# Storing the result of a two-layer cross-head convolution in 64 stores of 1 MB instead of 128 of 512 KB

## The chip, the cores and the metric

The kernel runs on one core of a Trainium2 chip. The metric is the time of one execution on the device in microseconds, as the median of several runs. The engines that matter are PE (matrix multiplications, with PEld loading its weights), DVE, ACT and POOL (element-wise work) and SP, which here only issues transfers. All transfers go through one queue of the core's 16 DMA engines.

## What is computed

The input x has 16 channels of 1024 rows (t) by 1024 columns (s), all in f32. Two layers of the same form follow each other, each with its own weights:

```
wI  = w + eye(16)
ret = einsum('MTS,MN->NTS', x, wI)                      # channels mixed
hq  = einsum('MTS,TIM->ITS', x, qw1);  ret += einsum('ITS,TIM->MTS', hq, qw2)   # rank 2, weights by row
hk  = einsum('MTS,SIM->ITS', x, kw1);  ret += einsum('ITS,SIM->MTS', hk, kw2)   # rank 2, weights by column
ret += x * qdd[t] + x * kdd[s]
```

So each layer applies a 16 x 16 matrix that depends on the row (T) plus one that depends on the column (S) to the channels. 64 MB are read and 64 MB are written.

## The kernel before

The image is worked on in 8 blocks (`BLOCKS`) of 128 rows. A block lies in SBUF as 16 chunks (`CHUNKS`) of 8 rows; a chunk is 128 partitions x 1024 f32, which is 4 KB in each partition and 512 KB in all. X holds the block's input and later the result of the first layer, Y holds sums on their way. Each layer has a pass by rows (T) and a pass by columns (S). The names in the code are t1 and s1 for the passes of the first layer, s2 and t2 for those of the second.

PE goes through them in a fixed order. For block k there is first the S stage: 16 groups of s1 (line 748) with those of s2 (line 767) two groups behind. Then comes the T stage: for each o in 0 to 15 the t2 products of output chunk o (line 796, two groups) and, right behind, t1 of chunk o of the next block k+1 (line 725). After t1 of chunk 15 the next block's S stage begins. PE waits for `x_loaded[j]` before t1 of chunk j (line 712). In the last block there is no t1, as there is no further block.

ACT moves the t1 sums from PSUM to Y (line 454) and the s2 sums to X (line 462). For each output chunk it also copies two half-tiles of X into OUT, which swaps the two halves of the partitions (`cross`, line 486). DVE adds the s1 sums to Y (line 614), makes every second weight tile of t2 (line 243) and adds the t2 sums into OUT in two instructions per chunk (`add_rows`, line 638), the second of which needs the crossed copies. POOL makes other weight tiles.

OUT has 4 slots (`OUT_SLOTS`); output chunk o uses slot o % 4. Before ACT's crossing of chunk o (line 483) and before DVE's first add of it (line 621) each waits until the store of chunk o - 4 has landed. Each slot has a semaphore `stored[n]`.

SP issues everything in program order. In the T stage (`t_phase`, line 319) it waits for each o until the adds of output chunk o are done, stores it (line 265), and loads chunk o + 3 of the next block (line 261, `SLACK` is 3) into the place that this output chunk has freed. After o = 11 it also issues the two stores of the next block's products of row weights (line 281, 128 KB each in runs of 64 bytes) and a load of row parameters (line 277); then follow o = 12, whose load is that of chunk 15, and the stores 13 to 15. Chunks 0 to 2 of the next block are loaded in the S stage (line 317), where nothing is stored; 16 loads of row weights RT are issued there as well (line 284).

Output chunk o holds rows of chunk (o + 3) % 16 (`t2_chunk`).

Of the kernel before, what the change touches and what calls it, by code (L numbers as in the profile page):

```python
# [4 lines left out]
P = 128  # L5
CH = 16
T, S = 1024, 1024
HALVES = 2
HALF = P // HALVES
PARTS = HALF // CH  # L10
EIGHTHS = HALVES * PARTS
COLS = S // EIGHTHS
WIDE = COLS // HALVES
ROWS = 128
BLOCKS = T // ROWS
RANK = 2
LAYERS = 2
PAIR = 2
PAIRS = ROWS // PAIR
CHUNK = 8  # L20
CHUNKS = ROWS // CHUNK
CHUNK2 = CHUNK // PAIR
SLACK = 3
# [5 lines left out]
PER_CHUNK = CHUNK // FEW  # L29
# [3 lines left out]
OUT_SLOTS = 4  # L33
# [16 lines left out]
QUARTERED_LAST = ()  # L50
PARAMS = 2 * RANK * CH + CH
DMA = 16
FLAT = CHUNK * COLS
BANK = 512
T1_COPIES = 2
# [5 lines left out]
def cross_conv_kernel(nc, x, first_rows, row_params, col_left, col_right0, col_right1, w, products, out):  # L61
# [15 lines left out]
    with ctx:  # L77
# [3 lines left out]
        def sem(name):  # L81
            return ctx.enter_context(nc.semaphore(name))
# [4 lines left out]
        OUT = sb("OUT", [P, OUT_SLOTS, CHUNK2, COLS, PAIR])  # L87
# [62 lines left out]
        a_done = sem("a_done")  # L150
        b_full = sem("b_full")
        b_done = sem("b_done")
        stored = [sem(f"stored{n}") for n in range(OUT_SLOTS)]


        def t1_groups(k):
# [21 lines left out]
        def t2_done(k):  # L178
            return (S1_ADDS * GROUPS + T2_GROUPS) * k + S1_ADDS * GROUPS
# [32 lines left out]
        def t2_chunk(o):  # L212
            return (o + SLACK) % CHUNKS
# [45 lines left out]
        def _(sp):  # L259
            def load_x(k, j):  # L260
                sp.dma_start(rows_of(X, k, j).rearrange("q a s c -> q (a s c)"),  # L261
                             x[bass.ds(k * CHUNKS + j, 1)].rearrange("b q v -> (b q) v")).then_inc(x_loaded[j], DMA)

            def store(k, o):
                sp.dma_start(out[bass.ds(k * CHUNKS + t2_chunk(o), 1)].rearrange("b q v -> (b q) v"),  # L265
                             OUT[:, o % OUT_SLOTS].rearrange("q a s c -> q (a s c)")
                             ).then_inc(stored[o % OUT_SLOTS], DMA)

            def load_right(h):

                for p in range(EIGHTHS):
                    sp.dma_start(KR1[h][CH * p:CH * (p + 1)].rearrange("q i s n -> q (i s n)"),  # L272
                                 col_right1[h, p:p + 1].broadcast_to([CH, RANK * SIDE * CH])
                                 ).then_inc(right_loaded[1 + h], DMA)

            def load_q(step):
                sp.dma_start(QP[:, :, :].rearrange("q l v -> q (l v)"),  # L277
                             row_params[bass.ds(step, 1)].rearrange("b t v -> (b t) v")).then_inc(q_loaded, DMA)

            def store_products(place, src, signal):  # L280
                sp.dma_start(products[bass.ds(place, 1)].rearrange("b c t n -> (b t) c n"), src).then_inc(signal, DMA)  # L281

            def load_part(place, l, p, first_row, rows, signal):
                sp.dma_start(RT[CH * p:CH * (p + 1), l, first_row:first_row + rows].rearrange("q t n -> q (t n)"),  # L284
                             products[bass.ds(place, 1), :, first_row:first_row + rows]
                             .rearrange("b c t n -> (b c) (t n)")).then_inc(signal, DMA)

# [30 lines left out]

            def t_phase(k, more, params):
                for o in range(CHUNKS):  # L320
                    sp.wait_ge(b_done, t2_done(k) + PER_CHUNK * (o + 1))
                    store(k, o)
                    if more and o + SLACK < CHUNKS:
                        load_x(k + 1, o + SLACK)
                    if more and o == PROD_STORE:
                        sp.wait_ge(prod_ready, LAYERS * (k + 2))
                        for l in range(LAYERS):
                            store_products(LAYERS * (k + 1) + l, PROD[:, l, 0], prod_stored)
                        if params:
                            load_q(k + 2)  # L330
# [118 lines left out]
        @block.scalar  # L449
        def _(act):  # L450
            def t1_copies(k, j):
                act.wait_ge(a_full, t1_groups(k) + j + 1)
                for h in range(HALVES):
                    nc.scalar.activation(  # L454
                        rows_of(Y, k, j)[:, :, WIDE * h:WIDE * (h + 1), :].rearrange("q a s c -> q a c s"),
                        PA[HALVES * (j % RING) + h][:, :].rearrange("q (a c s) -> q a c s", a=CHUNK2, c=PAIR),
                        ACT.Copy).then_inc(a_done, 1)

            def s2_copies(k, g):
                act.wait_ge(a_full, s2_groups(k) + g + 1)  # L460
                for i in range(HALVES):
                    nc.scalar.activation(columns_of(block_of(X, k), slice(0, P), WIDE * i + NARROW * g),  # L462
                                         by_columns(PA[HALVES * (g % RING) + i][:, :]), ACT.Copy
                                         ).then_inc(a_done, 1)

            def s1_matrices(k, g):

                act.wait_ge(b_full, s1_groups(k) + g - SLOTS + 1)
                if first(k):
                    act.wait_ge(mask_ready, 3)  # L470
                    act.wait_ge(right_done, UNITS)
                slot = WB[:, g % SLOTS].rearrange("q (t a n) -> q t a n", t=INDEX, a=PARTS)
                for a in range(PARTS):
                    nc.scalar.activation(slot[:, :, a, :], RS[:, 0, INDEX * g:INDEX * (g + 1)], ACT.Copy,  # L474
                                         scale=mask[:, a:a + 1]).then_inc(wb_act, 1)

            def cross(k, o):

                if o in quartered(k):
                    return  # L480
                if not (first(k) and o < OUT_SLOTS):

                    act.wait_ge(stored[o % OUT_SLOTS], DMA * (CHUNKS // OUT_SLOTS * k + o // OUT_SLOTS))
                lower, upper = slice(0, HALF), slice(HALF, P)
                for dst, src in ((lower, upper), (upper, lower)):
                    nc.scalar.activation(OUT[dst, o % OUT_SLOTS, :, WIDE:COLS, :],  # L486
                                         rows_of(X, k, t2_chunk(o))[src, :, WIDE:COLS, :], ACT.Copy
                                         ).then_inc(crossed, 1)

            def base(l):  # L490

                for n in range(CH):
                    nc.scalar.activation(RS[:, l, :, n:n + 1].rearrange("q s n -> q (s n)"), KL[:, l, RANK], ACT.Identity,
                                         bias=WI[:, l, n:n + 1], scale=delta[:, n:n + 1]).then_inc(base_ready, 1)

            def block_copies(k, more):
                s1_matrices(k, SLOTS)
                for g in range(GROUPS):
                    if g + LAG + SLOTS in ACT_S1:
                        s1_matrices(k, g + LAG + SLOTS)  # L500
                    s2_copies(k, g)

                act.wait_ge(a_done, t1_done(k + 1))
                cross(k, 0)
                for o in range(CHUNKS):
                    if more:
                        t1_copies(k + 1, o)
                    if o + 1 < CHUNKS:
                        cross(k, o + 1)

            act.wait_ge(wi_ready, LAYERS)
            for l in range(LAYERS):
                base(l)
            for j in range(CHUNKS):
                t1_copies(0, j)
            block_copies(0, True)
            with act.Fori(1, BLOCKS - 1) as k:
                block_copies(k, True)
            block_copies(BLOCKS - 1, False)

        @block.vector
        def _(dve):
# [94 lines left out]
            def add_rows(k, o):  # L617
                dve.wait_ge(b_full, t2_groups(k) + PER_CHUNK * (o + 1))
                if not (first(k) and o < OUT_SLOTS):

                    dve.wait_ge(stored[o % OUT_SLOTS], DMA * (CHUNKS // OUT_SLOTS * k + o // OUT_SLOTS))
                slot, place = OUT[:, o % OUT_SLOTS], rows_of(X, k, t2_chunk(o))
                banks = PBS[:, HALVES * (o % RING):HALVES * (o % RING + 1)]
                for i in range(HALVES):
                    def rows(chunk):
                        return chunk[:, :, WIDE * i:WIDE * (i + 1), :].rearrange("q a s c -> q a c s")

                    if o in quartered(k):
                        sums = banks[:, i].rearrange("q (a c s) -> q a c s", a=CHUNK2, c=PAIR)
                    else:  # L630
                        sums = banks.rearrange("q b (a c s) -> q (b a) c s", a=FEW2, c=PAIR
                                               )[:, :, :, WIDE * i:WIDE * (i + 1)]
                    other = place
                    if i and o not in quartered(k):

                        dve.wait_ge(crossed, crossings(k, o + 1))
                        other = slot
                    nc.vector.tensor_tensor(rows(slot), sums, rows(other), ALU.add).then_inc(b_done, 1)  # L638
# [247 lines left out]
```

## Time and profile before

| | |
|---|---|
| median of 3 runs | 790.45 us (783.79 to 791.59) |
| profiled execution | 784.83 us, its span 783.0 us |
| PE busy | 687.3 us (88%) |
| DVE, ACT, POOL busy | 541.5, 499.1, 485.2 us (69%, 64%, 62%) |
| mean granted PE clock | 0.962 of full speed |
| DMA | 159.08 MB, mean 203 GB/s; the queue's packets take 63.3% of the 16 engines' span |
| chain that ended last | PE 65%, SP's queue 9%, DMA 9%, issue 8%, DVE 7% |

The chain's share says which work stood on the path that set the end. A wait is told by who waited and what released it. "Issue" is time in which an engine waited for nothing that the profile shows. The landing time of a transfer is counted from its issue by SP until all of it has landed. In the slices of the span the DMA's busy share swings between nearly 0 and 9 tenths: the T stages carry the loads of x and all the stores, the S stages little.

### The profile page before, as it was taken

The page shows a single profiled execution, that of the slowest core. Times are in us where ns is not written, and L with a number is a line of the kernel's source. Part 1 is how long each engine was busy: PE and PEld are TensorE (multiplying, and loading weights), DVE is VectorE, ACT ScalarE, POOL GpSimd, SP SyncE. Part 2 cuts the span into 40 slices and gives each one's busy share as a digit, 9 for nine tenths or more (in the row PEclk, how much of TensorE's full clock was granted, in tenths as well). Part 3 has the DMA queues.
Part 4 walks back from the last instruction along what each step waited for, and adds up shares of the span by engine and source line. Part 5 has one row for each costly group of instructions (what it writes and reads, how often), then busy time and mean ns, then how long its engine had stood idle before and what let it go on. Part 6 is the DMA issues. An engine that isn't in the chain of part 4 may idle for free.

```text
span 783.0 us, 42554 instructions
## 1 busy us (share of the span) xinstructions
PE 687.3 (88%) x18448; PEld 634.9 (81%) x18448; DVE 541.5 (69%) x769; ACT 499.1 (64%) x929; POOL 485.2 (62%) x456
## 2 busy tenths in 40 slices
PE   7378899888998999988998989979999789988976
PEld 2368889887887888978897988969989779988975
DVE  4375667475875758756785667757786567957797
ACT  7246577565776667755776657757777557765753
POOL 2257777566665766657765666647866467656632
PEclk9669999999999999989999899999999999999999
DMA  7982559942896529855499437975399545992055
GB/s 165 204 283 58 138 200 340 270 112 77 310 324 198 132 83 349 269 185 144 157 339 265 126 111 269 315 231 129 111 355 277 175 132 188 335 272 61 9 210 215
DMA packets 78567, 159.08 MB, mean 203 GB/s; under 512 B 42048, under 2 KB 43072, under 8 KB 76224
## 3 DMA queue, kind: packets, MB, share of 16 engines
q1 hardware_dynamic: 78408, 156.59, 63.3%
q8 instruction: 146, 2.39, 1.3%
q14 instruction: 13, 0.11, 0.0%
HBM read 87.22 MB, written 69.34 MB: 200 GB/s over the span
## 4 chain that ended last, share of the span: by engine, by line
PE 65%; SPq 9%; DMA 9%; issue 8%; DVE 7%; ACT 0%; DVEq 0%; ACTq 0%
PE PB L796 22%; PE PB L748 15%; PE PA L767 14%; PE PA L725 14%; DMA X<-in_x_dram 8%; SPq L281 5%; DVE OUT L638 3%; DVE WB L243 2%; DVE Y L614 2%; SPq L277 1%; SPq L265 1%; SPq L272 1%; SPq L284 1%; DMA products<-RT 1%; SPq L261 1%
## 5 line engine op out<-in xcount | busy, mean ns | idle before, releaser
L796 PE MATMUL PB<-Y,WB 128*128 128x128 f32 x2048 | 268.8, 281 | 9.5 <-DVE OUT L638 8.2
L796 PEld LDWEIGHTS PB<-Y,WB 128*128 128x128 f32 x2048 | 242.4, 188 | 22.7 <-issue 15.4
L614 DVE TENSOR_TENSOR Y<-PB,Y 128x512 f32 (+1 forms) x256 | 165.1, 689 | 107.4 <-PE PB L748 88.2
L454 ACT ACTIVATE Y<-PA 128x512 f32<-128x512 f32 (+1 forms) x256 | 146.5, 631 | 132.3 <-PE PA L725 132.1
L243 POOL TENSOR_TENSOR WB<-RT,mask 128x512 f32<-128x512 f32 x128 | 143.0, 1117 | 111.4 <-PE PB L796 107.7
L725 PE MATMUL PA<-X,WA 64*64 64x64 f32 x8192 | 165.2, 231 | 45.5 <-DMA X<-in_x_dram 24.9
L462 ACT ACTIVATE X<-PA 128x512 f32 (+1 forms) x256 | 140.4, 606 | 98.4 <-PE PA L767 98.3
L725 PEld LDWEIGHTS PA<-X,WA 64*64 64x64 f32 x8192 | 146.1, 143 | 64.9 <-DMA X<-in_x_dram 27.5
L235 POOL TENSOR_TENSOR WA<-RS,mask 128x512 f32<-128x512 f32 x128 | 133.5, 1043 | 85.4 <-PE PA L767 53.2
L748 PE MATMUL PB<-X,WB 64*64 64x128 f32 x4096 | 162.8, 281 | 19.7 <-issue 14.1
L235 POOL TENSOR_TENSOR WA<-RT,mask 128x512 f32<-128x512 f32 x128 | 140.2, 1098 | 61.6 <-PE PA L725 27.2
L486 ACT ACTIVATE OUT<-X 64x512 f32<-64x512 f32 (+1 forms) x256 | 161.1, 629 | 20.3 <-DMA out_dram<-OUT 13.7
L767 PE MATMUL PA<-Y,WA 64*64 64x128 f32 x4096 | 157.9, 274 | 10.8 <-issue 10.6
L243 DVE TENSOR_TENSOR WB<-RT,mask 128x512 f32<-128x512 f32 x128 | 111.5, 871 | 75.7 <-PE PB L796 43.4
L748 PEld LDWEIGHTS PB<-X,WB 64*64 64x64 f32 x4096 | 140.1, 138 | 26.4 <-issue 26.3
L767 PEld LDWEIGHTS PA<-Y,WA 64*64 64x64 f32 x4096 | 136.2, 133 | 16.4 <-issue 15.2
L638 DVE TENSOR_TENSOR OUT<-PB,X 128x512 f32<-128x512 f32 x128 | 88.2, 689 | 19.9 <-PE PB L796 18.1
L235 POOL TENSOR_TENSOR WB<-RS,mask 128x512 f32<-128x512 f32 x64 | 72.1, 1126 | 30.1 <-PE PB L748 16.8
L638 DVE TENSOR_TENSOR OUT<-PB,OUT 128x512 f32<-128x512 f32 x128 | 87.3, 682 | 0.4
L474 ACT ACTIVATE WB<-RS,mask 128x128 f32<-128x128 f32 x128 | 41.0, 396 | 19.4 <-PE PB L748 19.3
L235 DVE TENSOR_TENSOR WB<-RS,mask 128x512 f32<-128x512 f32 x32 | 31.4, 984 | 13.0 <-PE PB L796 12.9
L565 DVE TENSOR_TENSOR PROD<-QP 128x256 f32<-128x256 f32 x32 | 31.3, 983 | 11.3 <-DMA QP<-in_rows_dram 11.3
(33 smaller groups left out, 87.4 us busy)
## 6 DMA issues: line engine op xcount, KB each, us to landing
X<-in_x_dram SPq DMA_DIRECT2D x128, 512.0 KB, 5.6
out_dram<-OUT SPq DMA_DIRECT2D x128, 512.0 KB, 4.4
RT<-products SPq DMA_DIRECT2D x120, 128.0 KB, 3.3
products<-PROD SPq DMA_DIRECT2D x16, 128.0 KB, 7.7
Y<-in_right_dram SPq DMA_DIRECT2D x8, 128.0 KB, 8.5
X<-in_right_dram SPq DMA_DIRECT2D x8, 128.0 KB, 11.3
RT<-products SPq DMA_DIRECT2D x8, 96.0 KB, 5.0
QP<-in_rows_dram SPq DMA_DIRECT2D x8, 80.0 KB, 3.9
```

The source lines that it names most:

```text
L235: engine.tensor_tensor(dst.rearrange("q (t a n) -> q t a n", t=count, a=PARTS), r, m, ALU.mult).then_inc(ready, 1)
L243: engine.tensor_tensor(dst.rearrange("q (t p n) -> q t p n", t=FEW, p=EIGHTHS), r, m, ALU.mult).then_inc(ready, 1)
L454: nc.scalar.activation(rows_of(Y, k, j)[:, :, WIDE * h:WIDE * (h + 1), :].rearrange("q a s c -> q a c s"), PA[HALVES * (j % RING) + h][:, ...
L462: nc.scalar.activation(columns_of(block_of(X, k), slice(0, P), WIDE * i + NARROW * g), by_columns(PA[HALVES * (g % RING) + i][:, :]), ACT.Copy
L474: nc.scalar.activation(slot[:, :, a, :], RS[:, 0, INDEX * g:INDEX * (g + 1)], ACT.Copy, scale=mask[:, a:a + 1]).then_inc(wb_act, 1)
L486: nc.scalar.activation(OUT[dst, o % OUT_SLOTS, :, WIDE:COLS, :], rows_of(X, k, t2_chunk(o))[src, :, WIDE:COLS, :], ACT.Copy).then_inc(cros ...
L614: nc.vector.tensor_tensor(at, by_columns(PB[HALVES * (g % RING) + h]), at, ALU.add).then_inc(b_done, 1)
L638: nc.vector.tensor_tensor(rows(slot), sums, rows(other), ALU.add).then_inc(b_done, 1)
L725: last = nc.tensor.matmul(PA[HALVES * (j % RING) + h][part(o), WIDE * r:WIDE * (r + 1)], matrix(WA[:, j % SLOTS], h, r), rows_of(X, k, j)[ ...
L748: last = nc.tensor.matmul(PB[HALVES * (g % RING) + h][part(o), ROWS * v:ROWS * (v + 1)] .rearrange("q (a c) -> q a c", c=PAIR), matrix(WB[ ...
L767: last = nc.tensor.matmul(PA[HALVES * (g % RING) + i][part(h ^ i), ROWS * v:ROWS * (v + 1)] .rearrange("q (a c) -> q a c", c=PAIR), matrix ...
L796: last = nc.tensor.matmul(PB[g % SLOTS][:, COLS * r:COLS * (r + 1)], WB[:, g % SLOTS, P * r:P * (r + 1)], rows_of(Y, k, t2_chunk(o))[:, (i ...
```

## The change

The store of an even output chunk is left out, and after each odd one both leave together: two neighbouring slots of OUT, 8 KB in each partition, go to one place of 1 MB in the output, whose layout has the two chunks side by side. There are two `stored` semaphores in place of four, one per pair of slots. The crossing and the first add of chunk o now wait until the pair that used the same two slots before has landed, for even and odd o alike. SP still waits at an even o where it has a load to issue there, and issues that load without a store ahead of it. The rearranging of the output on the host is no part of the time.

```
-        stored = [sem(f"stored{n}") for n in range(OUT_SLOTS)]
+        stored = [sem(f"stored{n}") for n in range(OUT_SLOTS // TWO)]
...
             def store(k, o):
-                sp.dma_start(out[bass.ds(k * CHUNKS + t2_chunk(o), 1)].rearrange("b q v -> (b q) v"),
-                             OUT[:, o % OUT_SLOTS].rearrange("q a s c -> q (a s c)")
-                             ).then_inc(stored[o % OUT_SLOTS], DMA)
+                slot = o % OUT_SLOTS
+                sp.dma_start(out[bass.ds(k * (CHUNKS // TWO) + o // TWO, 1)].rearrange("b q v -> (b q) v"),
+                             OUT[:, slot - TWO + 1:slot + 1].rearrange("q e a s c -> q (e a s c)")
+                             ).then_inc(stored[slot // TWO], DMA)
...
             def t_phase(k, more, params):
                 for o in range(CHUNKS):
-                    sp.wait_ge(b_done, t2_done(k) + PER_CHUNK * (o + 1))
-                    store(k, o)
+                    if o % TWO or more and o + SLACK < CHUNKS:
+                        sp.wait_ge(b_done, t2_done(k) + PER_CHUNK * (o + 1))
+                    if o % TWO:
+                        store(k, o)
                     if more and o + SLACK < CHUNKS:
                         load_x(k + 1, o + SLACK)
...
-                    act.wait_ge(stored[o % OUT_SLOTS], DMA * (CHUNKS // OUT_SLOTS * k + o // OUT_SLOTS))
+                    act.wait_ge(stored[o % OUT_SLOTS // TWO], DMA * (CHUNKS // OUT_SLOTS * k + o // OUT_SLOTS))
...
-                    dve.wait_ge(stored[o % OUT_SLOTS], DMA * (CHUNKS // OUT_SLOTS * k + o // OUT_SLOTS))
+                    dve.wait_ge(stored[o % OUT_SLOTS // TWO], DMA * (CHUNKS // OUT_SLOTS * k + o // OUT_SLOTS))
...
-    out = nc.dram_tensor("out_0_dram", (BLOCKS * CHUNKS, P, FLAT), _mybir.dt.float32, kind="ExternalOutput").ap()
+    out = nc.dram_tensor("out_0_dram", (BLOCKS * CHUNKS // TWO, P, TWO * FLAT), _mybir.dt.float32, kind="ExternalOutput").ap()
```

## Rows read from the trace of the kernel before

**Rows 1.** The page's DMA issues: line, count, KB each, median us to landing.

```profile
out_dram<-OUT SPq DMA_DIRECT2D x128, 512.0 KB, 4.4
```

**Rows 2.** Chain of waits, end of block 3's T stage: start us, us, what.

```profile
417.63 3.81 SPq L281
...
424.10 0.34 SPq L265
...
424.64 6.14 DMA X<-in_x_dram
```

**Rows 3.** PE's waits from 100 us on: total us, times, longest.

```profile
PE PA L725 <- DMA X<-in_x_dram: 19.2, 8, 3.7
```

**Rows 4.** PE's timeline, t1 of chunk 15, four of seven boundaries: start, us, [idle before].

```profile
246.08 1.17 PE L725 MATMUL PA<-X,WA 64*64 64x64 f32 x64 [1.55 <-DMA X<-in_x_dram]
...
430.82 1.99 PE L725 MATMUL PA<-X,WA 64*64 64x64 f32 x64 [3.73 <-DMA X<-in_x_dram]
...
523.35 1.18 PE L725 MATMUL PA<-X,WA 64*64 64x64 f32 x64 [2.20 <-DMA X<-in_x_dram]
...
702.14 1.61 PE L725 MATMUL PA<-X,WA 64*64 64x64 f32 x64 [2.37 <-DMA X<-in_x_dram]
```

**Rows 5.** DVE's timeline, the first column add behind three of these boundaries.

```profile
248.81 2.51 DVE L614 TENSOR_TENSOR Y<-PB,Y 128x512 f32 x4 [2.83 <-ACT Y L454]
...
434.77 1.29 DVE L614 TENSOR_TENSOR Y<-PB,Y 128x512 f32 x2 [6.22 <-PE PB L748]
...
705.58 3.94 DVE L614 TENSOR_TENSOR Y<-PB,Y 128x512 f32<-128x512 f32 x6 [4.36 <-PE PB L748]
```

**Rows 6.** Two stretches of 3 us: busy time by engine, PEclk, DMA share, GB/s.

```profile
246.00:249.00 3.00, 2.92 (x128) 2.70 (x128) 0.19 (x1) 1.69 (x5) 1.04 (x1) 1.00 0.79 302
...
431.00:434.00 3.00, 3.00 (x92) 3.00 (x95) 0.00 (x0) 1.13 (x2) 1.04 (x1) 0.50 0.67 274
```

**Rows 7.** Line 261: the load at 424.64, then S-stage loads from 80 and from 540 us.

```profile
DMA to landing us min/median/max: 6.1/6.1/6.1
...
DMA to landing us min/median/max: 3.4/4.1/5.0
...
DMA to landing us min/median/max: 4.1/5.5/5.8
```

**Rows 8.** SP's timeline, the store of o = 12 in block 5.

```profile
604.22 1.09 SPq L265 DMA_DIRECT2D out_dram<-OUT  x1
```

**Rows 9.** Block 3, o = 7: SP's issues, the load's landing, PE's t1(10), ACT's crossing(10).

```profile
403.20 0.35 SPq L265 DMA_DIRECT2D out_dram<-OUT  x1
403.74 0.35 SPq L261 DMA_DIRECT2D X<-in_x_dram  x1
...
DMA to landing us min/median/max: 4.9/4.9/4.9
...
410.98 1.17 PE L725 MATMUL PA<-X,WA 64*64 64x64 f32 x64
...
410.27 1.28 ACT L486 ACTIVATE OUT<-X 64x512 f32<-64x512 f32 x2
```

**Rows 10.** Block 3, o = 1: SP's load of chunk 4, its landing, PE's t1(4).

```profile
384.59 0.35 SPq L261 DMA_DIRECT2D X<-in_x_dram  x1
...
DMA to landing us min/median/max: 6.5/6.5/6.5
...
391.43 1.18 PE L725 MATMUL PA<-X,WA 64*64 64x64 f32 x64
```

**Rows 11.** Last block's T stage: queue over 743 to 783 us, line 265's landings, DVE's adds.

```profile
q1 hardware_dynamic: 2304, 8.39, 51.9%
...
DMA to landing us min/median/max: 2.6/2.6/4.2
...
744.71 0.68 DVE L638 TENSOR_TENSOR OUT<-PB,OUT 128x512 f32<-128x512 f32 x1
...
752.37 0.68 DVE L638 TENSOR_TENSOR OUT<-PB,OUT 128x512 f32<-128x512 f32 x1
```

More of the change, by code:

```diff
@@ L52 @@
 DMA = 16
+TWO = 2
 FLAT = CHUNK * COLS
@@ L877 @@
     r = _run(nc, [arrays], core_ids=[0])
-    got = _np.asarray(r.results[0]["out_0_dram"]).reshape(BLOCKS, CHUNKS, HALVES, PARTS, CH, CHUNK2, HALVES, WIDE, PAIR)
+    got = _np.asarray(r.results[0]["out_0_dram"]).reshape(BLOCKS, CHUNKS // TWO, P, TWO, FLAT).transpose(0, 1, 3, 2, 4)
+    got = _np.roll(got.reshape(BLOCKS, CHUNKS, P, FLAT), SLACK, axis=1)
+    got = got.reshape(BLOCKS, CHUNKS, HALVES, PARTS, CH, CHUNK2, HALVES, WIDE, PAIR)
     swapped = got.copy()
```

## The prediction, made before the changed kernel ran

> **What bounds the kernel now.** The page's chain gives PE 65% and DMA with SP's queue 18%, so I read the chain of waits in order of time next and looked where it leaves PE. It does so at the end of each T stage but the last. In block 3 SP is held for 3.8 us by a store of row-weight products, reaches the store of output chunk 12 at 424.10 and issues the load of chunk 15 behind it at 424.64; that load needs 6.1 us [rows 2, 7]. Chunk 15 is the last that the next block's first row pass needs, and PE stands idle for 3.73 us until it is there [rows 4]. PE's waits say how much this is worth in all: from 100 us on it waited 19.2 us for x, in 8 waits [rows 3]. One is a wait of 0.4 us inside a T stage; seven are these boundaries, together 18.9 us, the smallest 1.55 and 2.20, the other five 2.4 to 3.7 (four of the seven are shown) [rows 4].
>
> Then I read the clock. After the stall of 3.73 us the granted clock was 0.50 (1.2 GHz), after that of 1.55 it stayed at 1.00 (2.4 GHz) [rows 6]. The 64 matmuls of t1(15) took 1.99 and 1.17 us there, 1.18 after the stall of 2.20 and 1.61 after that of 2.37 [rows 4]. What a low clock costs is read where DVE's first column add follows: it started 2.73 us after t1(15) at full clock, 3.95 us at half, and 3.44 us in the last boundary [rows 4, 5]. So three more boundaries look like block 3's, and cold starts cost 4 x 1.2 + 0.7 = 5.5 us.
>
> Everywhere else in a T stage PE runs without a gap and the DMA engines are nearly full: the question there is only whether something becomes late.
>
> **The change part by part.** *The store ahead of the load of chunk 15 goes.* That load is issued where the store was, 0.54 us sooner [rows 2]. And it needn't move 512 KB of store first. What those cost: in the last block 16 stores took 51.9% of 16 engines for 40 us, 332 us of packets, thus 332 / 16 / 16 = 1.3 us per store [rows 11]. From 6.1 us the landing falls to 4.8 by that count. Loads with no store near them, three in each S stage, took 4.1 us in the middle, with a median of 5.5 in the worst stage [rows 7]. I take 4.4, nearer to the lone loads as the queue is almost empty at 424. The load then lands 0.54 + 6.1 - 4.4 = 2.2 us sooner. In the last two boundaries the store's own issue took 1.09 us, since SP was still pressed by the products' many runs [rows 8]; the load will meet this itself, and I count only the 1.3 us. Where the stall is shorter than the gain it caps it. Sum: 3 x 2.2 + 1.6 + 2.2 + 2 x 1.3 = 13.0 us. Bounds: only the earlier issue, 7 x 0.5 = 3.5 us less any backlog; at the other end the whole 18.9 us.
>
> *The clock.* The stalls that are left are 0.7 to 1.6 us, and rows 6 shows the clock held after 1.55. So I add the 5.5 us, with bounds 0 and 5.5. The Trainium skill, "TensorE: Matmul & The Clock Gate", section "Part 1: The HAM clock gate", says that the throttled state is the default and that sustained activity releases it; by that rule, the trace agrees, the gain comes; had the falls another cause, it would be 0.
>
> *Stores of even chunks come later.* They leave one chunk, 3.1 us, later, and the pair takes 1.3 us more to land. A store's median landing was 4.4 [rows 1], so a pair's is about 5.7. ACT's crossing of chunk 10 started 7.07 us after the store of chunk 7, which is now the store it waits for [rows 9]: 1.4 us are left, and behind it DVE's second add and PE's t2 two chunks later have cover of their own. If the landing took 7 us or more, ACT would slip, then DVE's add, then PE. Cost 0, bounds 0 to 1 us per T stage.
>
> *Loads at odd o now stand behind 1 MB.* The load of o = 7 landed 4.9 us after its issue, and PE came to it 7.24 us after the issue [rows 9]; 1.3 us more still fits. In a crowded stretch the landing took 6.5 us with PE at 6.84 [rows 10], and 1.3 more would stall it by 1 us. But there the queue was backed up: the store now absent from before the even load is done in the same queue a moment later, and as long as the engines never idle the odd load ends when it did. An idle moment comes only where the backlog is below 1.3 us, and there the cover is long. I take 1 us in all. Bounds: 0, and 1 us in each of 7 stages.
>
> *The pair of o = 11 stands before the products.* If it made SP's issue of these slower, the load of chunk 15 would lose what it won. By the same argument 0; at most 1.3 us per boundary, 9 us.
>
> *Loads at even o, 6 per stage,* lose the store ahead of them; this removes the 0.4 us wait at most. The 64 store issues that go, at 0.34 us, and their waits lie on SP, which idles between chunks: 0.
>
> *The last block.* It has no loads. DVE sets its pace. The pair of chunks 0 and 1 leaves after the add at 744.71 ends at 745.39, lands 2.6 + 1.3 = 3.9 us later, crossings take 1.3 more, and the add that needs them is at 752.37, 7.0 us after [rows 11]: hidden. ACT's waits grow there, to nobody's cost. But the very last store is of 1 MB with nothing behind it: +1.3 us.
>
> Sum: 13.0 + 5.5 - 1.0 - 1.3 = 16.2 us less than this execution's 784.8, which gives 768.6. The four executions shown lie at 783.8, 784.8, 790.5 and 791.6, mean 787.7; a median of runs is 3 us above the profiled one. I forecast 772.
>
> **The rivals.** *The load of chunk 15 lands hardly sooner.* For it: its 6.1 us are 2.0 more than a lone load's 4.1, of which the store ahead explains 1.3 at most, and a lone stage's median reached 5.5 [rows 7]; right behind it 1 MB of stores still follows. Then the gain is 3.5 - 1 - 1.3, about 1 us, and the clock still falls: 786 to 789. Against: stores of 1.3 us each stand between the two counts. Chance 0.2.
>
> *Slower: odd loads late.* 1 MB of writes in one piece ahead of a load. Its place is PE's wait at t1 of even chunks; it decides where such a load takes over 7.2 us from issue in the steady part. At the crowded row's price, 1 us for each of 6 odd loads in 7 stages, 42 us come on top: 772 + 42 = 814; at half of it 793, after the gain at the boundaries. For it: DMA is nearly full in the T stages and rows 10 has only 0.3 us to spare. Against: the bytes are the same, and rows 9 has 2.3 us. Chance 0.12.
>
> *Instruction supply takes over.* "Issue" holds 8% of the chain, and PE's program is fetched by the same engines. While PE stalls for x its fetches run ahead; without the stall they may come just in time. Half of the 13.0 goes: 772 + 6.5 = 778 or 779. The Trainium skill, "DMA: Bandwidth & Descriptors", section "Queues, rings and completion order", says that a DMA engine changes queues only between whole packets; runs of 8 KB would make a fetch wait longer. No row shows that here. Chance 0.08.
>
> That it doesn't do what it says, 64 stores of 1 MB, has nothing for it in the diff.
>
> **How the numbers follow.** The forecast's case has 0.6, with its own range 763 to 781: at 763 all stalls and cold starts are gone (787.7 - 18.9 - 5.5 + 1.3 = 764.6, or 761.8 against the profiled time), at 781 half of the gain is. The range reaches up to 788 for the first rival, and leaves out the slower one and a little below. 1% of 790.45 is 7.9 us, about what a measurement of this kernel tells from no change. Faster takes the forecast (0.6) and the fetch rival (0.08); same takes the first rival (0.2); slower the second (0.12).
>
> **What would show it.** The issues: 64 stores of 1024 KB. PE's waits for x: 19.2 us down to about 6, and t1(15) preceded by 0 to 1.6 us. The load of chunk 15: about 4.4 us to landing. PEclk 1.00 behind most boundaries, first column add 2.7 us behind t1(15). In the T stages PE without gaps; if there are waits for x of about 1 us at even chunks, the slower rival holds. The last store lands in 3.9 us. I am wrong if chunk 15 still needs 6 us, or if the time between boundaries (PE's, from one t1(15) to the next) grows by what the boundary gave.

## The result, and where the time went

The changed kernel took 821.59 us (median of 4 runs, 817.48 to 823.01) beside 789.42 us (783.79 to 791.59) for the one before: a ratio of 1.042, 95% interval 1.037 to 1.047. It is slower by 32 us; I had forecast 772. The profiled execution has a span of 820.9 us, against 783.0.

The page of the kernel after: busy time, the chain that ended last, and the issues of transfers (its lines are shifted: t1 is line 730, s1 753, s2 772, t2 801).

```profile
PE 691.7 (84%) x18448; PEld 636.3 (78%) x18448; DVE 535.3 (65%) x769; ACT 498.8 (61%) x929; POOL 483.6 (59%) x456
...
PE 70%; issue 13%; DVE 6%; DMA 6%; SPq 4%; ACT 1%; DVEq 0%; POOL 0%; ACTq 0%; POOLq 0%
...
X<-in_x_dram SPq DMA_DIRECT2D x128, 512.0 KB, 5.6
out_dram<-OUT SPq DMA_DIRECT2D x64, 1024.0 KB, 5.1
```

The edit does what it says: 64 stores of 1 MB, whose median landing is 5.1 us where a single one had 4.4 [rows 1]. DMA and SP fell from 18% to 10% of the chain, as I wanted, but "issue" rose from 8% to 13%, and PE with it.

PE's waits from 100 us on say the same in microseconds. First the kernel after, then the one before, whose wait for x was [rows 3].

```profile
PE PA L730 <- issue: 30.4, 20, 3.8
PE PB L753 <- issue: 14.3, 16, 2.1
PE PA L772 <- issue: 13.4, 14, 2.9
PE PB L801 <- issue: 13.2, 10, 2.8
...
PE PA L730 <- DMA X<-in_x_dram: 3.9, 3, 2.3
```

```profile
PE PB L748 <- issue: 13.9, 14, 2.0
...
PE PA L767 <- issue: 7.4, 10, 2.0
PE PA L725 <- issue: 7.1, 8, 2.2
...
PE PB L796 <- issue: 0.3, 1, 0.3
```

The waits for x fell from 19.2 to 3.9 us. The load of chunk 15 is late at two of the seven boundaries only, by 0.7 and 2.3 us. But in the T stages (t1 and t2) PE waited 30.4 + 13.2 = 43.6 us for nothing that the profile names, where it had waited 7.1 + 0.3 = 7.4 us. In the S stages these waits went from 21.3 to 27.7 us.

Measured from the first t1 group of a T stage to the group of chunk 15, the seven T stages took 390.7 us instead of 360.1, though the old figure has 18.9 us of waiting for chunk 15 in it. The S stages between them took 2.9 us more, the rest 4 us. So the loss sits in the T stages: without the waits for chunk 15 they took 387.8 us instead of 341.2. Of these 46.6 us more, 36 are the waits just counted, and the t2 matmuls were busy for 276.3 us instead of 268.8.

**What PE waits for there.** PE runs a long straight program. It does not come through the queue that SP fills (q1) but through a second one on the same DMA engines: queue q8, "instruction", fetched it in 146 packets of 16 KB, 2.39 MB, in both kernels. Here is one of the gaps, in the chain of the kernel after, and then the DMA queues in the 4.9 us ahead of PE's stop and in the gap itself.

```profile
338.26 2.01 PE PB L801 x16
340.27 0.96 PE PA L730 x44
341.23 3.08 issue
344.31 0.46 PE PA L730 x11
```

```profile
q1 hardware_dynamic: 676, 1.46, 99.8%
...
q1 hardware_dynamic: 3546, 0.25, 98.7%
q8 instruction: 1, 0.02, 2.6%
```

The first queue line is 336.3 to 341.2 us, the last two 341.3 to 344.3. Before the gap the data queue filled the 16 DMA engines (99.8%) and no instruction packet started. In the gap one did, from 341.66 to 342.90 us (the one before it had started at 334.60), and PE went on 1.4 us after its end. This is no single case. From 100 us on the kernel after has 42 issue waits of over 0.6 us, 64.7 us together, and every one of them ended 1.2 to 1.9 us after the end of an instruction packet; a moment taken at random lies so in 14% of the time. In the kernel before it was 20 of 20.

That the packets themselves came late can be read too, as PE's program is the same in all kernels but for the counts it waits for. For each of the 68 packets of the T stages I took, over the traces of 14 kernels, the smallest number of matmuls that PE had begun when the packet started, and then, in each trace, the time from the last of these matmuls to the packet's start. The mean of this delay was 1.3 us before and 2.0 us after the change (the difference is 0.7, with a standard error of 0.2). In the S stages it was 0.5 and 0.7 us. So PE's program arrives just in time, and in the T stages, where the data queue fills the DMA engines, it arrives later since the change. When PE asked for a packet no row shows.

For the gap shown, SP's timeline gives what stood in the data queue: a pair's store at 335.11, a load and the two product stores.

```profile
335.11 0.35 SPq L268 DMA_DIRECT2D out_dram<-OUT  x1
335.66 0.35 SPq L262 DMA_DIRECT2D X<-in_x_dram  x1
336.30 5.07 SPq L284 DMA_DIRECT2D products<-PROD  x2
```

Behind this gap the granted clock was at the lower of its two levels (1.2 GHz), 0.50 in the third column from the end:

```profile
345.20:348.20 3.00, 3.00 (x18) 2.78 (x21) 0.69 (x1) 2.02 (x4) 0.70 (x2) 0.50 0.86 310
```

Between 100 us and the last few microseconds the trace after has seven stretches at that level. Each began within 1.6 us of the end of an issue wait of 1.6 to 3.8 us, and five lie in T stages. None began at a wait for chunk 15; before the change five of six did.

### The profile page after: what moved, and what is told of

Read it like the earlier page. It is cut to its first block, busy times and chain, and to the rows that moved or that the text cites. A ratio compares the mean times of both kernels' runs of the same rounds, so it can differ in the third digit from the quotient of the medians.

```text
span 820.9 us, 42404 instructions
## 1 busy us (share of the span) xinstructions
PE 691.7 (84%) x18448; PEld 636.3 (78%) x18448; DVE 535.3 (65%) x769; ACT 498.8 (61%) x929; POOL 483.6 (59%) x456
## 3 DMA queue, kind: packets, MB, share of 16 engines
q1 hardware_dynamic: 69192, 156.58, 61.7%
q8 instruction: 146, 2.39, 1.3%
## 4 chain that ended last, share of the span: by engine, by line
PE 70%; issue 13%; DVE 6%; DMA 6%; SPq 4%; ACT 1%; DVEq 0%; POOL 0%; ACTq 0%; POOLq 0%
PE PB L801 26%; PE PA L730 16%; PE PB L753 14%; PE PA L772 14%; DMA X<-in_x_dram 4%; DVE Y L619 2%; DVE WB L244 2%; DVE OUT L643 1%; SPq L284 1%; SPq L275 1%; SPq L287 1%; DMA out_dram<-OUT 1%; DMA products<-RT 1%; ACT OUT L491 1%; SPq L280 0%
## 5 line engine op out<-in xcount | busy, mean ns | idle before, releaser
L801 PE MATMUL PB<-Y,WB 128*128 128x128 f32 x2048 | 276.3, 286 | 21.6 <-issue 13.2
L801 PEld LDWEIGHTS PB<-Y,WB 128*128 128x128 f32 x2048 | 248.9, 192 | 34.7 <-issue 27.5
L772 PE MATMUL PA<-Y,WA 64*64 64x128 f32 x4096 | 162.8, 273 | 16.4 <-issue 16.3
L753 PEld LDWEIGHTS PB<-X,WB 64*64 64x64 f32 x4096 | 138.2, 132 | 32.2 <-issue 32.1
L772 PEld LDWEIGHTS PA<-Y,WA 64*64 64x64 f32 x4096 | 139.6, 132 | 22.6 <-issue 21.4
```

What stands on the lines that cost most here:

```text
L753: last = nc.tensor.matmul(PB[HALVES * (g % RING) + h][part(o), ROWS * v:ROWS * (v + 1)] .rearrange("q (a c) -> q a c", c=PAIR), matrix(WB[ ...
L772: last = nc.tensor.matmul(PA[HALVES * (g % RING) + i][part(h ^ i), ROWS * v:ROWS * (v + 1)] .rearrange("q (a c) -> q a c", c=PAIR), matrix ...
L801: last = nc.tensor.matmul(PB[g % SLOTS][:, COLS * r:COLS * (r + 1)], WB[:, g % SLOTS, P * r:P * (r + 1)], rows_of(Y, k, t2_chunk(o))[:, (i ...
```

## The experiments

Two questions: what about the pair makes PE's instructions late, and what became of the gain at the boundaries. To the first there were three answers when the runs began: A, the size of one transfer; B, the length of a run in it; C, the bytes that stand in front of a fetch at once, however they are cut. Each time is a median beside runs of the kernel before on the same chip, and each ratio is against those. "T waits" are PE's issue waits of t1 and t2 from 100 us on, and "fetch delay" is the mean delay of the T stages' instruction packets, as above. Both are read from one execution of each kernel.

### Two transfers, or one in shorter runs, at the same moments

two_512 stores the pair as two transfers of 512 KB:

```
+                for e in range(TWO):
+                    sp.dma_start(out[bass.ds(k * (CHUNKS // TWO) + o // TWO, 1), :, FLAT * e:FLAT * (e + 1)]
+                                 .rearrange("b q v -> (b q) v"), OUT[:, slot - TWO + 1 + e]...)
```

> Stores leave in pairs as in the changed kernel, at the same moments, but as two transfers of 512 KB in runs of 4 KB. Theory A (PE's instruction fetches wait behind one large transfer's share on a DMA engine, so the size of one transfer decides): PE's issue waits in the T stages fall from 43.6 us back to about 7, the wait for the load of chunk 15 stays gone, some 775 to 785 us. Theory B (the length of a run, 8 KB instead of 4 KB, decides): the same, 775 to 785. Theory C (the bunching decides, 1 MB of stores at once after a pause): still about 820 us. Rival D (odd loads late, as I priced it before): still about 820, with waits for x, of which the changed kernel shows only 3.9 us.

Measured: 805.51 us, ratio 1.014 (1.006 to 1.022).

one_4k keeps one transfer of 1 MB but cuts each partition's 8 KB in two runs:

```
+                sp.dma_start(out[bass.ds(k * CHUNKS + o - 1, TWO)].rearrange("b q v -> q b v"),
+                             OUT[:, slot - TWO + 1:slot + 1].rearrange("q e a s c -> q e (a s c)")
```

> One transfer of 1 MB per pair, at the same moments, but each partition's 8 KB go out as two runs of 4 KB (the output laid out in chunks as before). Theory A (size of the transfer): as slow as the changed kernel, about 820 us, PE's issue waits in the T stages about 40 us. Theory B (length of a run): 775 to 785 us and issue waits of about 7. Theory C (bunching): about 820.

Measured: 826.23 us, ratio 1.040 (1.032 to 1.048).

PE's waits, first two_512 (t1 is line 732, t2 803), then one_4k (730, 801):

```profile
PE PA L732 <- issue: 19.4, 23, 2.3
...
PE PA L732 <- DMA X<-in_x_dram: 5.8, 6, 1.3
...
PE PB L803 <- issue: 5.1, 6, 1.5
```

```profile
PE PA L730 <- issue: 32.4, 25, 2.8
...
PE PB L801 <- issue: 12.3, 8, 2.5
...
PE PA L730 <- DMA X<-in_x_dram: 0.7, 1, 0.7
```

T waits are 24.5 and 44.7 us, the fetch delays 1.7 and 2.0 us. The run length (B) falls: with 4 KB runs and one transfer nothing is better than the 43.6 us of the changed kernel. The size of the transfer (A) has an effect of some 16 us, but not all of it: two_512 is still slower than before.

halves_8k was to tell the same from the other side, with two transfers of 64 partitions each and runs of 8 KB:

```
+                for h in range(HALVES):
+                    half = slice(HALF * h, HALF * (h + 1))
+                    sp.dma_start(out[bass.ds(k * (CHUNKS // TWO) + o // TWO, 1), half]..., OUT[half, slot - TWO + 1:slot + 1]...)
```

> The pair leaves as two transfers of 512 KB, each of 64 partitions with runs of 8 KB, at the same moments. Theory A (size of the transfer): 775 to 785 us. Theory B (length of a run): about 820 us. Theory C (bunching): about 820 us.

Measured: 839.85 us, ratio 1.057 (1.048 to 1.065). The slowest of the four, as none of the theories that still stand says. Its profile shows another ill (t1 is line 732, t2 803):

```profile
q1 hardware_dynamic: 70216, 156.59, 67.6%
...
X<-in_x_dram SPq DMA_DIRECT2D x128, 512.0 KB, 7.0
...
PE PA L732 <- DMA X<-in_x_dram: 29.8, 22, 2.7
...
PE PA L732 <- issue: 20.5, 17, 3.0
...
PE PB L803 <- issue: 5.6, 7, 1.7
```

The same bytes took 67.6% of the engines, of a longer span, against 61.7%, loads landed in 7.0 us and PE waited 29.8 us for x. Stored by half the partitions, they hold the engines for longer; why is not settled. On A the run says two things: T waits are 26.1 us, near those of two_512, but the fetch delay is 1.9 us, near that of one transfer of 1 MB. So it decides nothing.

### The load of chunk 15 first, by itself

x15_first is the kernel before, with my main term alone:

```
+                    last = o + SLACK == CHUNKS - 1
+                    if not (more and last):
+                        store(k, o)
                     if more and o + SLACK < CHUNKS:
                         load_x(k + 1, o + SLACK)
+                    if more and last:
+                        store(k, o)
```

> The kernel before, with 128 stores of 512 KB, and one edit: at o = 12 the load of chunk 15 is issued ahead of the store. My prediction's term by itself: the load lands about 2 us sooner at each of 7 boundaries, waits for x fall from 19.2 us to 5 to 8, the clock holds in most: 771 to 778 us. If the fetches take what the loads give back: 783 or more.

Measured: 788.37 us, ratio 0.995 (0.992 to 0.999). PE's waits:

```profile
PE PB L752 <- issue: 23.3, 22, 1.9
PE PA L729 <- issue: 15.8, 18, 1.7
PE PA L771 <- issue: 10.6, 16, 1.8
...
PE PA L729 <- DMA X<-in_x_dram: 3.1, 5, 0.9
PE PB L800 <- issue: 0.7, 1, 0.7
```

This run shows what became of the gain. The waits for x fell to 3.1 us, 16 less, as I had worked out. The mean granted clock rose: 0.976 to 0.981 in its ten runs, 0.959 to 0.975 in the 13 of the kernel before beside them. But the issue waits of all four groups rose from 28.7 to 50.4 us. By place: in the 10 us behind the seven boundaries they rose from 1.5 to 10.5 us, in the T stages up to there from 7.3 to 12.9, the rest later in the S stages. While PE stalled for chunk 15 its program could catch up: in three of the seven stalls of the kernel before an instruction packet ended inside the stall. Without the stall PE meets its instruction supply at once, and 21.7 us of the one wait stand where 16 of the other were. The exact sum is partly chance: each trace is one execution, and that of the kernel before took 784.8 us, at the fast end of its runs, while the medians differ by 3.4 us in favour of x15_first.

### How small must a transfer be

four_256 sends the pair as four transfers of 256 KB.

```
+                part = FLAT // SPLIT
+                for e in range(TWO):
+                    for h in range(SPLIT):
+                        sp.dma_start(out[bass.ds(k * (CHUNKS // TWO) + o // TWO, 1), :,
+                                         FLAT * e + part * h:FLAT * e + part * (h + 1)]..., OUT[:, slot - TWO + 1 + e]...)
```

> The changed kernel's moments, but the pair's 1 MB goes out as four transfers of 256 KB (runs of 2 KB). One transfer of 1 MB gave 822 to 826 us, two of 512 KB gave 806. Theory A, mended (an instruction fetch waits behind the share of whole transfers on its DMA engine, so smaller transfers let it in sooner): below 806 us, 790 to 800, and PE's issue waits in the T stages below two_512's 24 us. Theory C (only the bytes in front of the fetch count, however they are cut): 806 us as with two, or more for the two extra issues. Then the 20 us between one transfer and two need another reason.

Measured: 793.34 us, ratio 1.007 (1.003 to 1.011). half_bytes stores only the odd chunk of each pair, in one transfer of 512 KB.

```
+                sp.dma_start(out[bass.ds(k * (CHUNKS // TWO) + o // TWO, 1), :, FLAT:TWO * FLAT]
+                             .rearrange("b q v -> (b q) v"), OUT[:, slot].rearrange("q a s c -> q (a s c)")
```

> The changed kernel's moments, but only the odd chunk of each pair is stored, in one transfer of 512 KB; the even chunk's store is left out of the computation's result, so 32 MB less are written. Theories A and C both say that the fetches then wait less: PE's issue waits in the T stages of 43.6 us fall below 10, and the time comes to 780 or less, since the DMA engines are free a third of the time. If the pairing harmed by something else than traffic in front of the fetches (a late crossing, SP's order), it stays at 800 or more.

Measured: 770.64 us, ratio 0.975 (0.967 to 0.983). The waits of four_256 (t1 is 735, t2 806), then those of half_bytes (731, 802):

```profile
PE PA L735 <- DMA X<-in_x_dram: 16.8, 21, 2.1
...
PE PA L735 <- issue: 8.4, 11, 1.2
...
PE PB L806 <- issue: 0.8, 1, 0.8
```

```profile
PE PA L731 <- issue: 4.5, 5, 2.0
...
PE PB L802 <- issue: 0.3, 1, 0.3
```

The same bytes at the same moments gave 44 us of T waits in one transfer, 24.5 in two and 9.2 in four; the times are 822, 806 and 793 us. That speaks against C in the form that only the bytes in front count. The fetch delays go the same way: 2.0, 1.7 and 1.2 us. With half of the store bytes left out, T waits are 4.8 us and the fetch delay is 0.9; so the pairing did no harm but by its traffic. This run halves the size of the transfer as well as the bytes, and can't tell one from the other. In four_256 PE waits 16.8 us for x, 10.6 of them for chunk 15 and 6.1 for even chunks: only these 6.1 are my slower rival, odd loads late behind stores.

The next three cut the transfers of x15_first, leaving all moments alone: st2 the stores, ld2 the loads of x, both2 both, each in two of 256 KB. The loads' edit stands here (LD_PARTS = 2); the stores' (ST_PARTS) has the same form.

```
+                part, rows = FLAT // LD_PARTS, CHUNK2 // LD_PARTS
+                for h in range(LD_PARTS):
+                    sp.dma_start(X[:, bass.ds(pair_at(k, j) + rows * h, rows), :, :]...,
+                                 x[bass.ds(k * CHUNKS + j, 1), :, part * h:part * (h + 1)]...).then_inc(x_loaded[j], DMA)
```

> x15_first (788.4 us) with every store and every load of x cut in two transfers of 256 KB along the row. Theory A: fetches wait less, PE's issue waits of 50 us fall by 10 to 20, 770 to 780 us. Theory C: no change, 787 to 790; runs of 2 KB instead of 4 KB could also make the transfers longer and it slower.

> x15_first with only the stores cut in two of 256 KB. Theory A with both directions alike: about half of what both2 gains, 778 to 785 us. If it is the stores alone that hold fetches up: the same as both2. Theory C: 787 to 790.

> x15_first (788.4 us) with only the loads of x cut in two. Cutting the stores alone gave 786.6, cutting both 774.3. Theory A with reads as the larger obstacle to a fetch: 775 to 780 us. If only both together help: 785 or more.

Measured: both2 774.34 us, ratio 0.979 (0.974 to 0.984); st2 786.62, 0.989 (0.981 to 0.998); ld2 772.87, 0.974 (0.969 to 0.980). Cutting the loads does it, and cutting the stores as well adds nothing that is told apart. st2 is thus against theory A, which gave it 778 to 785 us: a lone store of 512 KB cut in two brought nothing that is clear of noise, though 1 MB of stores cut in two and in four did. PE's waits in ld2, whose profiled execution took 779.8 us:

```profile
PE PB L756 <- issue: 21.0, 24, 1.5
PE PA L775 <- issue: 11.9, 15, 1.6
PE PA L733 <- issue: 8.2, 11, 2.0
...
PE PA L733 <- DMA X<-in_x_dram: 5.6, 6, 2.0
```

T waits fell from 16.5 us to 8.2, and the fetch delay from 1.5 to 1.2 us; in st2 they are 17.6 and 1.5. ld2 is the version that beats both kernels, by 2.6% (2.0 to 3.2) and 5.9%.

split_only cuts both in two but keeps the store of o = 12 ahead of the load of chunk 15 (both2 without the edit of x15_first).

> The kernel before in its own order (store 12 ahead of the load of chunk 15), with stores and loads cut in two of 256 KB. If the fetches' waits are what the stall at the boundary used to hide, both edits are needed together: waits for x at the boundaries stay at 15 to 19 us and the time is 780 to 787. If the cutting does it alone: 774 as both2.

Measured: 785.95 us, ratio 0.994 (0.991 to 0.998); waits for x of 22.9 us in 12 waits. The two edits are needed together: either one alone gives 0.5%, both give 2.1%.

both4 is both2 with ST_PARTS = LD_PARTS = 4, transfers of 128 KB.

> x15_first with every store and every load of x cut in four transfers of 128 KB (runs of 1 KB). Cut in two they gave 774 us. Theory A (an instruction fetch waits behind whole transfers' shares): another 3 to 8 us less, 766 to 772. If the shorter runs and the 8 issues per chunk on SP cost more than the fetches win, 775 or more. Theory C is spoken against by the two, four and one of the pair; if it held, 788.

Measured: 934.41 us, ratio 1.182 (1.176 to 1.189). SP can't issue 8 transfers per chunk in time: its loads (line 265) and stores (272) are 35% of the chain, given here by lines, and PE waits for x. From the first of a chunk's 8 issues to the end of the last it needs 4.8 us (median), with 4 in both2 2.3 us, and a chunk's turn is 3.1 us. So this run says nothing on how small a transfer should be for the fetches.

```profile
SPq L265 20%; SPq L272 15%; PE PB L760 14%; PE PA L779 13%; PE PB L808 5%; DMA X<-in_x_dram 4%; PE PA L737 3%; DVE OUT L650 3%; DVE WB L245 2%; DVE Y L626 1%; SPq L289 1%; SPq L280 1%; SPq L292 1%; SPq L285 1%; DMA products<-RT 0%
```

```profile
PE PA L737 <- DMA X<-in_x_dram: 129.1, 78, 3.0
```

### Lateness, and the loads of the changed kernel

What makes two_512 17 us slower than x15_first: that the even store comes a chunk late, or that two transfers stand there at once? late_one issues each store of x15_first one chunk later.

```
+                    if o and o != CHUNKS - SLACK - 1:
+                        store(k, o - 1)
...
+                    if o == CHUNKS - 1:
+                        store(k, o)
```

> x15_first with each store (512 KB, alone) issued one chunk later, behind the adds of the next chunk. The changed kernel makes even chunks' stores one chunk late and puts two together. If the lateness by itself costs (late crossings), 795 to 806 us and ACT waits for stores in the T stages. If two_512's 17 us over x15_first are due to the two stores being in front together, 786 to 790 us here.

Measured: 795.58 us, ratio 1.008 (1.003 to 1.013). DVE waited 20.2 us for stores and ACT 24.1 us, all of it ahead of the last block; in the last block ACT waited another 16.1 us for them. late_inner leaves the last block as it was.

```
+                    if not more:
+                        store(k, o)
+                    elif o and o != CHUNKS - SLACK - 1:
+                        store(k, o - 1)
...
+                    if more and o == CHUNKS - SLACK - 1:
+                        store(k, o - 1)
+                    if more and o == CHUNKS - 1:
+                        store(k, o)
```

> x15_first with each store of 512 KB issued one chunk later, in the first 7 blocks only; the last block as before. If two_512's 17 us over x15_first come from the two transfers in front of the fetches together: 786 to 791 us here, PE's issue waits as in x15_first, 50 us. If the lateness itself costs (crossings held up in the T stages): 795 us or more, with ACT and DVE waiting for stores ahead of the last block.

Measured: 797.51 us, ratio 1.012 (1.007 to 1.016). Its waits:

```profile
ACT OUT L493 <- DMA out_dram<-OUT: 21.0, 7, 4.8
DVE OUT L645 <- DMA out_dram<-OUT: 16.8, 6, 4.3
```

That is the stretch from 100 to 735 us, ahead of the last block. The store of chunk 11 now stands behind the products, and chunk 15, which takes its slot, is held up. In two_512 and in the changed kernel no engine waits for a store in that stretch. So late_inner is slow for a reason of its own, and the question is answered only in part: its issue waits of 43.6 us are not above x15_first's 50.4, nor its fetch delay of 1.3 us above 1.5, so lateness does not starve PE of instructions. That the two transfers together do is what is left, not what a run shows by itself.

after_ld2 is the changed kernel with its loads cut in two, by the edit of ld2.

> The changed kernel, stores of 1 MB, with every load of x cut in two of 256 KB. In x15_first this cut brought 15 us. Theory A (a fetch waits behind the share of each transfer in front of it, stores and loads alike): it helps here too, 805 to 815 us of 822. If a fetch is held up by the longest transfer alone: no change, 820 or more.

Measured: 804.02 us, ratio 1.022 (1.014 to 1.029); T waits 18.2 + 4.4 = 22.6 us instead of 43.6. The stores of 1 MB aren't all of it: about half of the loss (17.6 of 32 us) can be had back from the loads. The fetch delay fell from 2.0 to 1.5 us.

## Why the prediction was wrong, step by step

- **Step that failed: "The store ahead of the load of chunk 15 goes", 13.0 us, and with it "The clock", 5.5 us.** The mechanism was right. The load landed 4.2 to 6.2 us after its issue (mean 4.9; forecast 4.4), and the waits for x went from 19.2 to 3.9 us (forecast about 6). What failed is that the wait's end was counted as time won. x15_first priced it: 13.0 + 5.5 us forecast, about 4 us of 790 came out. The rest went into issue waits, 28.7 to 50.4 us. Of the 50 us between 772 and 821.6 this step is about 16 (x15_first took 788.4), and the next one the other 33.
- **Step that was missing from the sum.** I had instruction supply as a rival with a chance of 0.08 and priced it at half of the gain, 6.5 us. It could only give back what was won, as I drew it. In fact it takes more: 36 us of T waits beyond the 7.4 of before, as fetches start later behind one transfer of twice the size (fetch delay 2.0 us, with two of 512 KB 1.7, with four of 256 KB 1.2, before 1.3). The rows for it were there: "issue" on 8% of the chain and 28.7 us in PE's waits, which I read as small, and DMA engines nearly full in the same stages. "Everywhere else in a T stage PE runs without a gap" was misread as well: t1 had 8 issue waits there, 7.1 us together, the longest 2.2 us. The sign of being wrong that I had named is the one that came: from the first t1(15) to the last PE took 576.8 us instead of 549.0.
- **Loads at odd o.** Taken at 1 us. Of the 3.9 us of x waits one, of 1.0 us, is at an even chunk (4), the other two are chunk 15's: right. The rival that ended on the other side had the right sign and the wrong mechanism; 814 us was near 822 by chance. Its own mechanism shows in four_256 and halves_8k, with 6.1 and 19.5 us of waits at even chunks.
- **Even stores later.** Cost 0, and none is seen: no waits for stores ahead of the last block. The pair's landing was 5.1 us for 5.7 forecast.
- **The pair ahead of the products.** Cost 0 taken. In block 3's like SP needed 5.07 us for the two product stores, of which the second had taken 3.81 of 4.60 us before [rows 2]. Near: 0.5 us more.
- **The last block.** The last store was waited for 3.5 us, before 2.3: +1.2 us, forecast 1.3. Right.
- **The clock.** Behind the boundaries it held, as forecast: the first column add came 2.45 to 2.74 us after t1(15) in six of seven. But the mean was 0.966 to 0.980 over the four runs, no higher than the kernel before has in its runs (0.959 to 0.981): PE now stands still for its instructions, and the clock falls there.
- **The page on DMA queues.** The Trainium skill, "DMA: Bandwidth & Descriptors", section "Queues, rings and completion order", says that an engine changes queues only between whole packets. I read a packet as one run and saw harm in 8 KB runs; one_4k shows that the run length is not it. If a packet is a transfer's whole share on an engine, the trace agrees: a store of 512 KB keeps each engine for 1.3 us [rows 11], one of 1 MB thus for 2.6 by estimate, and the T waits go down with the size of the transfer at the same bytes and moments (44, 24.5, 9.2 us). That the fetch waits for just such a share was not measured, and st2, where cut stores changed nothing, does not bear it out. For maximum bandwidth the same page's "Rules for kernel authors" asks for 128 partitions and transfers of 1 MiB or more; here, where PE is the bound, loads of 256 KB gave the fastest kernel, and of the stores over all 128 partitions those of 1 MB the slowest.

## What to carry to other kernels

A wait that vanishes is worth what the next one in line leaves of it. When PE is fed by a long straight program, look at its issue waits beside the instruction queue before counting a stall as time to be had: a stall may be where instructions catch up. And where the DMA engines are full while PE is the bound, the size of one transfer is a cost to whoever shares the engines; cut what is bulky, loads too, and stop before the issuing engine becomes the limit.

## What I had not expected of the hardware

- 71 us of PE's time from 100 us on were issue waits, and all of those over 0.6 us ended with the arrival of instructions, in a kernel whose instruction fetches are 1.5% of the bytes (2.39 of 159 MB).
- The 4 KB or 8 KB length of a run made no difference that can be told (826 and 822 us); the size of the transfer did (T waits 43.6, 24.5, 9.2 us).
- The loads' size mattered more than the stores': cut in two they gave 15 us (788.4 to 772.9), the stores 2, which is not clear of noise. Why is open.
- The same 1 MB stored as two transfers of 64 partitions in 8 KB runs kept the engines longer than as one of 128 partitions: the queue's share was 67.6% of 840.8 us against 61.7% of 820.9. Open.
- SP issued 4 transfers per chunk of 3.1 us in 2.3 us (median) and 8 in 4.8 (both4, 934 us).
